# A decoder layer on one core: who inverts the softmax sums of the self-attention units

## The reference

```python
scores = jnp.einsum('bhqd,bhkd->bhqk', q, k) * scale
scores = jnp.where(masked[None, None], -jnp.inf, scores)   # j > i, or |i - j| > 32
attn = jax.nn.softmax(scores, axis=-1)
out = jnp.einsum('bhqk,bhkd->bhqd', attn, v)
```

## Time and profile before

| | |
|---|---|
| median of 3 runs | 399.0 us (398.82 to 399.34) |
| the profiled execution | 399.12 us |
| its span, first to last instruction | 397.3 us |
| PE busy | 96% |
| DVE busy | 73% |
| ACT busy | 54% |
| POOL busy | 43% |
| granted TensorE clock, mean | 1.000 |

### The profile page before, as it was taken

How to read it: one execution, slowest core, us unless ns; L and a number is a source line. 1 busy time by engine, 2 the same in 40 slices (tenths; PEclk the granted TensorE clock), 3 DMA queues, 4 the chain that set the end, 5 groups by cost and what they waited for, 6 DMA issues and landing times.

```text
span 397.3 us, 8280 instructions
## 1 busy us (share of the span) xinstructions
PE 383.3 (96%) x3080; PEld 316.9 (80%) x3080; DVE 288.4 (73%) x627; ACT 214.4 (54%) x549; POOL 170.5 (43%) x169
## 2 busy tenths in 40 slices
PE   8999999889999999999999999999999899999997
PEld 8768778767799777887789877887779779866795
DVE  4878922888769974689959977489877964685374
ACT  1464844588343852298453663187744746188330
POOL 5562779578511550178620450067831520066000
PEclk9999999999999999999999999999999999999999
DMA  6996441314032000351013000352004000200000
GB/s 196 346 374 188 145 130 55 117 43 99 3 104 70 2 2 29 132 152 55 2 68 106 2 2 26 107 147 60 2 2 158 2 2 3 79 2 0 28 0 28
DMA packets 21894, 30.48 MB, mean 77 GB/s; under 512 B 2528, under 2 KB 15712, under 8 KB 21600
## 3 DMA queue, kind: packets, MB, share of 16 engines
q1 hardware_dynamic: 21856, 29.96, 24.0%
HBM read 22.88 MB, written 7.08 MB: 75 GB/s over the span
## 4 chain that ended last, share of the span: by engine, by line
PE 65%; DVE 17%; POOL 7%; issue 6%; ACT 3%; POOLq 0%; DVEq 0%; ACTq 0%
PE ps L694 13%; PE ps L775 10%; PE ps L791 5%; PE ps L634 4%; PE ps L560 4%; DVE rope L1014 3%; POOL prob L1320 3%; PE ps L593 3%; DVE mx L1043 3%; DVE total L1057 3%; PE ps L655 3%; PE ps L569 3%; PE ps L552 2%; PE ps L553 2%; PE ps L556 2%
## 5 line engine op out<-in xcount | busy, mean ns | idle before, releaser
L1320 POOL TENSOR_TENSOR prob<-prob,inv 128x512 f32<-128x512 f32 x80 | 82.7, 1041 | 76.7 <-DVE inv L1063 76.7
L1464 ACT ACTIVATE prob<-ps,mx 128x128 f32<-128x128 f32 (+1 forms) x128 | 52.6, 427 | 18.0 <-DVE mx L1041 14.8
L694 PE MATMUL ps<-wo_sb,qs 128*128 128x256 f32 x256 | 59.8, 380 | 0.0
L1313 POOL TENSOR_TENSOR qs<-rope 128x512 f32<-128x512 f32 x31 | 39.6, 1277 | 37.8 <-DVE rope L1014 36.0
L634 PE MATMUL ps<-ident_sb,prob 128*128 128x128 f32 x320 | 49.8, 278 | 3.5 <-POOL prob L1320 3.1
L694 PEld LDWEIGHTS ps<-wo_sb,qs 128*128 128x128 f32 x256 | 46.9, 191 | 6.7 <-issue 1.6
L1479 ACT ACTIVATE pT<-ps 128x512 f32<-128x512 f32 x76 | 45.7, 602 | 10.2 <-PE ps L634 9.4
L1014 DVE TENSOR_TENSOR rope<-ps,trig_sb 64x512 f32<-64x512 f32 x70 | 48.1, 688 | 0.9
L634 PEld LDWEIGHTS ps<-ident_sb,prob 128*128 128x128 f32 x320 | 36.6, 141 | 12.1 <-POOL prob L1320 8.2
L1306 POOL TENSOR_TENSOR rstd<-vareps,power 128x1 f32<-128x1 f32 x24 | 13.1, 550 | 64.5 <-DVE vareps L993 64.2
L1041 DVE TENSOR_REDUCE mx<-ps 128x2 f32<-128x512 f32 (+1 forms) x48 | 32.8, 687 | 7.3 <-PE ps L614 6.6
(11 more groups left out here) (169 smaller groups left out, 805.6 us busy)
## 6 DMA issues: line engine op xcount, KB each, us to landing
k<-kx SPq DMA_DIRECT2D x32, 128.0 KB, 2.8
q<-qx SPq DMA_DIRECT2D x28, 128.0 KB, 2.5
work<-in_wgu SPq DMA_DIRECT2D x4, 512.0 KB, 8.1
wo_sb<-in_wo SPq DMA_DIRECT2D x1, 2048.0 KB, 13.7
vx<-pT SPq DMA_DIRECT2D x7, 256.0 KB, 2.7
wq_raw<-in_wqk SPq DMA_DIRECT2D x3, 512.0 KB, 8.9
vb<-vx SPq DMA_DIRECT2D x6, 256.0 KB, 4.2
vb<-vx SPq DMA_DIRECT2D x6, 224.0 KB, 4.7
```

What stands on the lines that cost most here:

```text
L694: mm = pe.matmul(half_banks(use, b)[:, 0, :], window_o[t][:, pair, r, :], wo_sb[:, pair, r, :], start=(pair == 0 and r == 0), stop=(pair = ...
L1313: pool.tensor_tensor(to, cos, sin, ALU.add).then_inc(s_sums, 1)
L1320: pool.tensor_tensor(p, p, inv[:, i % ND, 0:g].unsqueeze(2).broadcast_to([P, g, 512 // g]), ALU.mult).then_inc(s_norm, 1)
L1464: ins = act.activation(prob[:, i % ND, h * k:(h + 1) * k], ps[:, BANK_S + i % 2, h * k:(h + 1) * k], ACT.Exp, bias=mx[:, i % ND, h:h + 1], ...
```

## The change

POOL inverts the sums of the self-attention units itself: it waits for DVE's sum, raises `total` to the power of minus one (all 8 columns; a broadcast column `minus_one` is the exponent), waits for its own result on a new semaphore, and multiplies. DVE makes no reciprocal for these units, and its wait for the multiplication four units before now stands ahead of the sum. Cross units keep DVE's reciprocal; its semaphore now counts these alone.

```diff
+        minus_one = sb("minus_one", [P, 1])
+        s_pinv = sem("s_pinv")
@@ DVE, unit_sum(b, i)
                 dve.wait_ge(s_exp, u + 1)
+                if u >= ND:
+                    dve.wait_ge(s_norm, u - ND + 1)
                 if i < NQB:
                     dve.tensor_reduce(total[:, i % ND, 0:g],
                                       prob[:, i % ND, :].rearrange("p (g k) -> p g k", g=g),
                                       AX.X, ALU.add).then_inc(s_sum, 1)
-                    dve.wait_ge(s_sum, NQB * b + i + 1)
-                if u >= ND:
-                    dve.wait_ge(s_norm, u - ND + 1)
+                    return
                 dve.reciprocal(inv[:, i % ND, 0:g], total[:, i % ND, 0:g]).then_inc(s_inv, 1)
@@ POOL, unit_norm(b, i)
-                pool.wait_ge(s_inv, u + 1)
+                if i < NQB:
+                    n = NQB * b + i + 1
+                    pool.wait_ge(s_sum, n)
+                    pool.tensor_tensor(inv[:, i % ND, :], total[:, i % ND, :], minus_one[:].broadcast_to([P, 8]),
+                                       ALU.pow).then_inc(s_pinv, 1)
+                    pool.wait_ge(s_pinv, n)
+                else:
+                    pool.wait_ge(s_inv, XU * b + i - NQB + 1)
                 p = prob[:, i % ND, :].rearrange("p (g k) -> p g k", g=g)
@@ POOL, start
+            pool.memset(minus_one[:], -1.0)
             pool.memset(power[:], -0.5).then_inc(s_power, 1)
```

## The result

The changed kernel takes 421.27 us (median of 6 runs, 420.55 to 423.22) against 399.12 for the kernel before on the same chip (398.82 to 399.46): a ratio of 1.0553, 95% interval 1.0536 to 1.0570, or 22.1 us more. The forecast was 404.8 us, 5.7 more than before, with a range of 400.4 to 480.

What follows compares the result with a forecast made beforehand. PE, busy 96% of the span, was taken as the bound, with waits hanging on sum-to-multiplication latency. At T = 0.9 the batches add 2.0 + 1.55 + 0.95 + 1.2 = 5.7 us to 399.1: 404.8 us, range 400.4 to 480.

Steps and rivals of the forecast that it cites:

- What comes: On GpSimd, self-attention units: 32 powers of 128x8, each followed by a wait for its own semaphore, then the multiplication.
- T: Time of GpSimd's power of eight columns: taken as 0.9 us, 0.55 if paid once, 3.4 if paid for each column.
- 12 us for each us of T: Whole kernel: added time by the steps, 1.5 us at T = 0.55, 5.7 at 0.9, about 9.9 at 1.25.
- per column: Rival on GpSimd: each column pays the power, T = 3.4, pitch 4.5 us, 477 us total; T above 1.3 had chance 0.36.
- the rests: Rounding work in GpSimd's queue behind multiplications, 1.23 to 1.27 us each: batch 0 from unit 4, batch 1 units 6 and 7.
- the latency of 1.88 + T: Self-attention unit, from the sum's start on DVE to GpSimd's multiplication's end: 1.88 + T us, against 2.03 before.
- the own wait: GpSimd's wait for its own semaphore between power and multiplication: taken as 0.07 us.
- DVE's pitch where nothing holds it: DVE's time from unit to unit without the reciprocal, where PE doesn't hold it: 1.93 us, 0.18 saved a unit.
- DVE's relief not being wanted: Mid-stretch PE is already slower than DVE by 0.13 us a unit, so what DVE saves there isn't wanted.
- the moved wait costing nothing: DVE's wait for the multiplication four units back, moved ahead of the sum, costs nothing whenever GpSimd keeps up.
- the steps as a function of T: Batch-by-batch delays of the four self-attention stretches and what follows: 1.5 us at T = 0.55, 5.7 at T = 0.9.
- cheap inversion: Rival on GpSimd: exponent -1 takes T = 0.25, -0.95 us, 398.2 us; T of 0.4 and less, or slack miscounted: chance 0.12.

Runs made afterwards that it cites:

- k8_both: Changed kernel with DVE's reciprocal put back, GpSimd waiting for it and taking the power all the same: 421.61 us, ratio 1.0569 to the kernel before.
- k0_wait: Kernel before with DVE's wait for the multiplication four units back moved ahead of the sum, plus the tile `minus_one`: 398.33 us, ratio 0.9976.
- p1_pad: Kernel before with one more tile of one column that nothing uses: 398.27 us, ratio 0.9976.
- c0_none: Changed kernel without any power for the self-attention units and without GpSimd's wait for its own result: 397.38 us, ratio 0.9939 to the kernel before.
- c1_cols: Changed kernel with the power taken of one of the eight columns: 400.20 us, ratio 1.0008 to the kernel before.
- c4_cols: Changed kernel with the power taken of four of the eight columns: 406.13 us, ratio 1.0152 to the kernel before.
- m1_widths: Changed kernel with eleven extra powers and multiplications of 1 to 32 columns behind GpSimd's last inverse root: 421.68 us, one execution.

## Why the prediction was wrong, point by point

**The step that failed is the price of the power**, in "What comes": T = 0.9 with 50 ns for each further column. It is 1.65, with 157 ns. The row of one column was right, and the bounds of 0.55 and 3.4 held it, as the range did; the point between them was a guess toward the row nearest to it. The prediction's own sign of being wrong, a power over 1.3 us, is what came.

**A second step would have failed even with the right T:** the "12 us for each us of T", carried on to T = 1.25. At T = 1.65 that line gives 14.7 us more than before, where 22.1 were measured. It prices a latency, with GpSimd's pitch as the bound in batch 0 alone. Above T = 1.13 that pitch, T + 1.11, passes TensorE's 2.24 us in every batch. The prediction had the sum for that case, but used it only for the rival "per column": eight pitches of 2.76 are 22.1 us, less 17.8 is 4.3 in each of four batches, with 3.7 more in batch 0 and 1.2 in batch 1 for the rests: 22.0 us. The stretches bear it out one by one (7.7, 5.1, 4.2 and 4.4 us, and 0.8 behind that of batch 1, against 8.0, 4.3, 4.3 and 4.3, and 1.2). That the total agrees to 0.1 us is luck: the pitch was 2.72, and the extra tile and the clock are not in the sum.

**Right:** the latency of 1.88 + T (the sum starts at 133.88, the multiplication ends at 136.37 + 1.04 = 137.41: 3.53); the own wait (136.29 to 136.37, 0.08 against 0.07); DVE's pitch where nothing holds it (133.88 to 135.79, 1.91 against 1.93); DVE's relief not being wanted (k8_both); the moved wait costing nothing (k0_wait beside p1_pad); and the steps as a function of T up to 1.0 us, as follows.

**Right by luck in part:** c0_none, c1_cols and c4_cols came within 0.4 us of the times put down, but these took the kernel before as 399.1, and it was 399.46 on that chip. By the ratios the three are 2.4 us under it, 0.3 and 6.1 over it, where -1.5, +1.5 and +7.1 were put down: each about 1 us too low. The traces show where that lies. The four stretches sum to 92.3 us in the kernel before, and to 91.1, 93.9 and 99.6 in the three: -1.1, +1.7 and +7.4 us, the steps' own numbers within 0.4. The rest of the gain, 1.1, 0.6 and 0.1 us in these executions, lies behind the stretches, where p1_pad, whose stretches also sum to 92.3, gains 1.3 us with the unused tile alone. So a free inversion is worth some 1.1 us here, and a power of 0.55 us costs 1.7.

**Missed:** the clock in batch 0, 0.5 us in the profiled execution and nothing in k8_both's. I had the wait growing there, but not what the matmuls behind it may take.

**The rival "cheap inversion"** is out: -1 costs as much as -0.5. The Trainium skill's factor of 2 between GpSimd and VectorE (GPSIMD Engine Reference, section 3) is measured there on an addition; for this inversion the traces have 1.65 us against 0.20, a factor of 8. **The rival "per column"** was right in kind and wrong in price: a column costs 0.157, not 0.41 us, since 0.39 of the 0.55 us is paid once.

## What to carry to other kernels

Before an operation is moved to an engine for a shape that the trace doesn't show, have its slope: one row at one width says nothing of the next column, and here the slope was the whole result. An engine with idle time is no free place if its own pitch in that stage, old work and new, comes above that of the engine that bounds it; here the threshold was 2.24 us and one subtraction would have shown that a power above 1.13 us crosses it. A slope worked out below such a crossing doesn't hold above it. And when differences of 0.2% are read, give every variant the same tiles, compare it with the kernel before on the same chip, and look in the trace for the stage in which the difference lies.

## What the runs showed of the hardware that I had not expected

- GpSimd's power of 128 x w in float32 takes 0.39 + 0.157 w us (m1_widths, w = 1 to 32), whichever of the two exponents; its multiplication of 512 columns takes 1.04.
- One unused tile of 128x1 ahead of the others makes the kernel before 0.8 us faster (0.9976, 0.9964 to 0.9987), in runs of 12 equal matmuls on TensorE whose pitch is 1.36 us instead of 1.42. The mean granted clock is 1.00 in both. None of the three traces without such a tile has the shorter pitch in any stage, and all eleven with it have it in one to four of five.
- In the trace of the changed kernel TensorE's granted clock was 0.53 over the 6 us behind 2.7 us without a matmul; in the one trace in which matmuls that nothing reads fill that time it was 1.00. Two of the changed kernel's six executions have a mean of 1.000, so the fall doesn't come every time.
